# A third PSUM bank in the ring between TensorE and ScalarE, the turned outputs moved into the outputs' bank, and the values read where they were written

## What is computed

```python
q, k, v = to_heads(x @ Wq), to_heads(k), to_heads(v)      # 16 heads, 2048 x 64 each
sim = jnp.einsum('bid,bjd->bij', q, k) * scale
sim = sim + _cope(q, sim, pos_emb)
attn = jax.nn.softmax(sim, axis=-1)
out = jnp.einsum('bij,bjd->bid', attn, v)
return out @ Wout + b_out
```

## Time and profile before

| | |
|---|---|
| median of 3 executions | 2291.75 us (2290.97 to 2293.32) |
| the profiled execution, its own time | 2291.38 us |
| its span in the trace | 2289.5 us |
| busy share of the span: TensorE, ScalarE, VectorE, GpSimd | 97%, 77%, 71%, 17% |
| pairs of the attention | 128, up to about 1856 us of the span |

### The profile page before, as it was taken

The page is one execution under the profiler, slowest core; times in us unless marked ns, Lnnn a source line. Parts: engine busy times, 40 slices in busy tenths (PEclk is TensorE's granted clock), DMA queues, the critical chain, the costliest instruction groups (busy, mean ns, idle before and its releaser), DMA issues. The chain is left out here.

```text
span 2289.5 us, 53196 instructions
## 1 busy us (share of the span) xinstructions
PE 2226.8 (97%) x14577; PEld 1446.7 (63%) x14577; DVE 1633.4 (71%) x4269; ACT 1762.5 (77%) x3723; POOL 389.3 (17%) x673
## 2 busy tenths in 40 slices
PE   7999999999999999999999999999999879999997
PEld 5666666666666666666666666666665547777775
DVE  5888888888888888888888888888888811223232
ACT  5888888888888888888888888888888843455453
POOL 1111111111111111111111111111111101121121
PEclk9999999999999999999999999999999989999998
DMA  2010101010101010101010101010101021010100
GB/s 74 24 40 25 39 24 40 23 39 23 39 25 41 23 40 24 40 23 40 23 39 23 39 23 39 23 40 23 33 14 57 15 67 35 30 39 30 39 30 7
DMA packets 109392, 75.44 MB, mean 33 GB/s; under 512 B 28077, under 2 KB 105070, under 8 KB 109294
## 3 DMA queue, kind: packets, MB, share of 16 engines
q1 hardware_dynamic: 109294, 73.95, 11.6%
HBM read 14.33 MB, written 2.10 MB: 7 GB/s over the span
## 5 line engine op out<-in xcount | busy, mean ns | idle before, releaser
L842 DVE TENSOR_REDUCE mx<-Sc 128x1 f32<-128x1024 f32 (+1 forms) x512 | 568.0, 1130 | 245.1 <-PE Sc L632 244.8
L483 ACT ACTIVATE probsT<-rings 128x512 f32<-128x512 f32 x1024 | 554.1, 594 | 194.6 <-PE rings L640 194.4
L640 PEld LDWEIGHTS rings<-ident,probs 128*128 128x128 f32 x4096 | 437.0, 141 | 304.4 <-issue 103.1
L507 ACT ACTIVATE probs<-Sc,nbias 128x1024 f32<-128x1024 f32 x512 | 566.9, 1112 | 27.9 <-DVE nbias L852 27.9
L640 PE MATMUL rings<-ident,probs 128*128 128x128 f32 x4096 | 566.6, 281 | 3.0 <-ACT probs L507 2.5
L632 PE MATMUL Sc<-qk,q_now 64*128 64x512 f32 x2048 | 531.3, 616 | 10.5 <-ACT probs L507 9.1
L654 PE MATMUL out<-probsT,V_now 128*64 128x256 f32 x4096 | 498.3, 385 | 0.0
L805 DVE COPY_PREDICATED z<-mask,z 128x224 f32<-128x224 int16 (+5 forms) x768 | 393.3, 512 | 11.1
L375 POOL TENSOR_TENSOR prod<-cut,z 128x350 f32<-128x350 f32 x128 | 120.7, 943 | 1466.8 <-DVE z L817 1466.8
L654 PEld LDWEIGHTS out<-probsT,V_now 128*64 128x64 f32 x4096 | 271.4, 136 | 153.6 <-issue 42.5
L632 PEld LDWEIGHTS Sc<-qk,q_now 64*128 64x128 f32 x2048 | 177.5, 186 | 115.9 <-issue 100.6
(11 more groups left out here) (128 smaller groups left out, 2256.8 us busy)
## 6 DMA issues: line engine op xcount, KB each, us to landing
q_now<-qk SPq DMA_DIRECT2D x256, 64.0 KB, 2.0
xv<-xT SPq DMA_DIRECT2D x113, 128.0 KB, 2.2
q_far<-qk SPq DMA_DIRECT2D x256, 32.0 KB, 1.8
V_now<-V SPq DMA_DIRECT2D x16, 512.0 KB, 3.0
at<-attn SPq DMA_DIRECT2D x16, 512.0 KB, 3.2
probs<-in_x_dram SPq DMA_DIRECT2D x4, 512.0 KB, 5.5
wqk<-in_L_attn_Wq_dram SPq DMA_DIRECT2D x32, 64.0 KB, 2.1
xin<-in_x_dram SPq DMA_DIRECT2D x16, 128.0 KB, 2.8
```

The source lines that it names most:

```text
L483: nc.scalar.activation(probsT[:, u, 4 * s:4 * s + 4, :], ring[k % 2][:, :].rearrange("p (t q) -> p t q", q=P), ACT.Copy).then_inc(slot_out, 1)
L507: nc.scalar.activation(probs[:, u, cols], Sc[:, cols], ACT.Exp, bias=nbias[:, u:u + 1], accum_out=sums[:, u, half:half + 1]).then_inc(exp_ ...
L640: last = nc.tensor.transpose(ring[k % 2][:, j * P:(j + 1) * P], probs[:, u, (4 * s + j) * P:(4 * s + j + 1) * P], ident[:, :])
L842: nc.vector.tensor_reduce(mx[:, u, half:half + 1], Sc[:, cols], AX.X, ALU.max).then_inc(dve_unit, 1)
```

## The change

The ring gets the bank of `turns` as its third, and the turned outputs go to columns 256 to 383 of the bank of `out`. `SLOT_BANK` says which bank each of the ten slots uses, and `out_for_bank` how many slots must have been copied out before slot k may be filled. Since the turned outputs and the outputs now share a bank, `outputs(g - 1)` begins only when the turned outputs of the pair g - 2 have been scaled (`scaled`), and ScalarE scales them earlier: between its second and third copy of that group of slots. `V_now`, its copies and the semaphore `v_in` are gone: `outputs` takes its weights straight from `V`. The window waits for slot 4 of the pair in place of slot 5, and only the second transposes of the group behind it wait for `near_out`.

```diff
+SLOT_BANK = [0, 1, 2, 0, 1, 2, 2, 0, 1, 2]
+
+
+def out_for_bank(base, k, late=False):
+
+    if k < 3:
+        return base + ([0, -3, -1] if late else [-2, -1, 0])[k]
+    return base + [1, 2, 3, 6, 4, 5, 7][k - 3]
...
-        V_now = sb("V_now", [P, NT, C])
...
-        rings = pb("rings", [P, 2, BANK])
-        ring = [rings[:, i, :] for i in range(2)]
+        rings = pb("rings", [P, 3, BANK])
+        ring = [rings[:, i, :] for i in range(3)]
         out = pb("out", [P, BANK])
-        turns = pb("turns", [P, BANK])
+        turns = out[:, 2 * P:2 * P + 2 * C]
...
-                if head:
-
-                    wait_apart(sp, out_full, g, waited)
-                    load_values(g)
...
                 if not first:
-                    transposed(1, base, at.last)
+                    transposed(1, base, at.last, (0, 1))
+                    if not second:
+                        scale(g - 2, 0)
+                        scale(g - 2, 1)
+                    transposed(1, base, at.last, (2, 3))
                 exp_half(g, 0, 0)
                 exp_half(g, 0, 1)
-                if not first and not second:
-                    scale(g - 2, 0)
-                    scale(g - 2, 1)
...
-            def transposes(u, base, slots, s):
+            def transposes(u, base, slots, s, late=False):
                 k = slots[s]
-                pe.wait_ge(slot_out, base + k - 1)
+                pe.wait_ge(slot_out, out_for_bank(base, k, late))
...
                     if empty:
                         pe.wait_ge(halves_out, g)
-                    wait_apart(pe, v_in, g // PAIRS * 16 + 16, waited)
+                        wait_apart(pe, scaled, g * 2, waited)
...
-                    last = nc.tensor.matmul(out[half:half + C, 0:2 * P], V_now[:, token_tile(t), :],
+                    last = nc.tensor.matmul(out[half:half + C, 0:2 * P], V[:, keys % 4, token_tile(t), :],
...
                 if far:
-                    wait_apart(pe, slot_out, base + at.now[0], waited)
+                    wait_apart(pe, slot_out, base + at.last[2] + 1, waited)
                     window(g + 2, par if far_par is None else far_par)
...
+                transposes(0, base, at.now, 0)
                 if far:
                     wait_apart(pe, near_out, g * 2 + 6, waited)
-                transposes(0, base, at.now, 0)
                 transposes(0, base, at.now, 1)
```

More of the change, by code:

```diff
@@ L286, in _, with body @@
             weights(1)
-            def load_values(g):
-                sp.dma_start(V_now[:, :, :], V[:, (g // PAIRS) % 4, :, :]).then_inc(v_in, 16)
             sp.wait_ge(slot_out, 8 + 2 * PAIRS)
-            load_values(0)
-            def body(g, odd, late=False, first=False, tile=True, far=True, head=False, near=False):
+            def body(g, odd, late=False, first=False, tile=True, far=True, near=False):
                 base = slots_before(g, late)
@@ L343, in _ @@
             load_early(sp, A, A["ctx_in"])
-            body(LASTP, False, late=True, tile=False, head=True)
+            body(LASTP, False, late=True, tile=False)
             body(LASTP + 1, True, late=True, tile=False)
@@ L412, in _, with project @@
             act.wait_ge(dve_consts, 5)
-            def project(s, odd, base, k, alone=False):
+            def project(s, odd, base, k, bank, alone=False):
                 h, b = s // PAIRS, (s + 7) % PAIRS
                 act.wait_ge(slot_full, base + k + 1)
-                nc.scalar.activation(qk[:, h % 2, int(odd), bass.ds(b // 2 * STEP, STEP)], ring[k % 2][:, 0:STEP],
+                nc.scalar.activation(qk[:, h % 2, int(odd), bass.ds(b // 2 * STEP, STEP)], ring[bank][:, 0:STEP],
                                      ACT.Copy, scale=qk_scale[:, int(odd):int(odd) + 1])\
@@ L533, in body @@
                 if proj:
-                    project(g + PAIRS, not odd, base, at.qk, alone=not val)
+                    project(g + PAIRS, not odd, base, at.qk, SLOT_BANK[at.qk], alone=not val)
                 if val:
@@ L572, in _, with project @@
                 last.then_inc(slot_full, 1)
-            def project(s, odd, base, k, weights_at, alone=False):
+            def project(s, odd, out_before, bank, weights_at, alone=False):
                 b = (s + 7) % PAIRS
                 pe.wait_ge(w_in, weights_at)
-                pe.wait_ge(slot_out, base + k - 1)
+                pe.wait_ge(slot_out, out_before)
                 at = 0 if odd else C
                 for c in range(DC):
-                    last = nc.tensor.matmul(ring[k % 2][:, 0:STEP], wqk[:, c, at:at + 2 * C],
+                    last = nc.tensor.matmul(ring[bank][:, 0:STEP], wqk[:, c, at:at + 2 * C],
                                             xT[:, c, bass.ds(b * STEP, STEP)],
@@ L585, in project, with project_values @@
                 last.then_inc(slot_full, 2 if alone else 1)
[L587 removed]
+            def project_values(s, out_before, bank, ahead=False):
                 if not ahead:
                     pe.wait_ge(xv_in, (s - PAIRS) * 16 + 16)
[L591 removed]
+                pe.wait_ge(slot_out, out_before)
                 for i in range(2 if ahead else 1):
@@ L594, in project_values @@
                         tile = xT[:, c, (2 * s + i) * P:(2 * s + i + 1) * P] if ahead else xv[:, c, :]
-                        last = nc.tensor.matmul(ring[k % 2][:, i * 2 * C:(i + 1) * 2 * C],
+                        last = nc.tensor.matmul(ring[bank][:, i * 2 * C:(i + 1) * 2 * C],
                                                 tile, wv[:, c, :],
@@ L634, in logits, with outputs @@
                 last.then_inc(bank_full, 1)
-            def transposes(u, base, slots, s):
+            def transposes(u, base, slots, s, late=False):
                 k = slots[s]
-                pe.wait_ge(slot_out, base + k - 1)
+                pe.wait_ge(slot_out, out_for_bank(base, k, late))
                 for j in range(4):
-                    last = nc.tensor.transpose(ring[k % 2][:, j * P:(j + 1) * P],
+                    last = nc.tensor.transpose(ring[SLOT_BANK[k]][:, j * P:(j + 1) * P],
                                                probs[:, u, (4 * s + j) * P:(4 * s + j + 1) * P], ident[:, :])
                 last.then_inc(slot_full, 1)
-            def outputs(g, base, slots, tiles, empty=True):
+            def outputs(g, base, slots, tiles, keys, empty=True):
                 if tiles[0] == 0:
@@ L667, in body @@
             def body(g, odd, par, late=False, first=False, proj=True, val=True, far=True, far_par=None,
-                     second=False, new_keys=False):
+                     second=False, new_keys=False, late_before=False, keys=0):
                 base = slots_before(g, late)
@@ L677, in body @@
                 if not first:
-                    transposes(0, base, at.late, 2)
-                    transposes(0, base, at.late, 3)
+                    transposes(0, base, at.late, 2, late_before)
+                    transposes(0, base, at.late, 3, late_before)
                     wait_apart(pe, exp_done, g * 4, waited)
@@ L684, in body @@
                 if not first:
-                    transposes(1, base, at.last, 0)
+                    transposes(1, base, at.last, 0, late_before)
                     transposes(1, base, at.last, 1)
@@ L690, in body @@
                     transposes(1, base, at.last, 3)
-                    outputs(g - 1, base, at.last, range(EARLY_TILES), empty=not second)
+                    outputs(g - 1, base, at.last, range(EARLY_TILES), keys, empty=not second)
                 if far:
-                    wait_apart(pe, slot_out, base + at.now[0], waited)
+                    wait_apart(pe, slot_out, base + at.last[2] + 1, waited)
                     window(g + 2, par if far_par is None else far_par)
@@ L730, in _ @@
             head(LASTP, 1, late=True, proj=False, val=False)
-            body(G - 2, False, 1, late=True, proj=False, val=False, far=False)
-            body(G - 1, True, 1, late=True, proj=False, val=False, far=False)
-            base, at = slots_before(G, True), Slots()
+            body(G - 2, False, 1, keys=H - 1, late=True, proj=False, val=False, far=False, late_before=True)
+            body(G - 1, True, 1, keys=H - 1, late=True, proj=False, val=False, far=False, late_before=True)
+            base, at, late_before = slots_before(G, True), Slots(), True
             pe.wait_ge(exp_done, 4 * G)
-            transposes(0, base, at.late, 2)
-            transposes(0, base, at.late, 3)
-            transposes(1, base, at.last, 0)
+            transposes(0, base, at.late, 2, late_before)
+            transposes(0, base, at.late, 3, late_before)
+            transposes(1, base, at.last, 0, late_before)
             transposes(1, base, at.last, 1)
@@ L741, in _ @@
             transposes(1, base, at.last, 3)
-            outputs(G - 1, base, at.last, range(NT))
-            pe.wait_ge(scaled, 2 * (G - 1))
+            outputs(G - 1, base, at.last, range(NT), H - 1)
             turns_of(G - 1)
```

44 lines of the change are left out of this document (23 added, 21 removed).

## The result

The changed kernel takes 2308.53 us, the median of four executions (2308.16 to 2310.65), against 2291.36 us (2290.72 to 2293.32) before, measured beside it: a ratio of 1.0072, with a 95% interval of 1.0059 to 1.0085. It is slower by 17 us. 2307 us were forecast. The profiled span grew by 16.7 us, from 2289.5 to 2306.2.

What follows compares the result with a forecast made beforehand. TensorE was taken to bound the kernel; outputs waiting for the scalings would cost 124 x 0.125 = 15.5 us, all else nothing, so 2291.75 + 15.5 = 2307 us. The range was 2294 to 2324, the forecast's own 2298 to 2319.

Steps and rivals of the forecast that it cites:

- TensorE sets the pace: First 112 pairs: TensorE busy 599.88 of 600 us, so delaying one of its matmuls lengthens the 14.19 us pair equally.
- The two real waits of the ring: Weight loads for slots 4 and 5 wait for ScalarE's copies; a third bank saves 0.13 us a pair, alone 16 us.
- Only the later of two times counts: Outputs start at the later of transposes done, about 1002.75, and scalings done, 1003.02; the third bank's saving is no separate term.
- The scalings are the later: Chain from turns through ScalarE's scalings to first outputs: 0.14 us late, taken as 0.125 a pair over 124 pairs, 15.5 us.
- 0.40 from turns to scaling: Step from the turns' end to ScalarE's first scaling, with two register instructions behind the wait: taken as 0.40 us.
- its bounds: Turns to first scaling: 0.11 us from the last pair with constant addresses, 0.45 from the projected queries and keys copy.
- The wake-up of TensorE: Step from the end of ScalarE's scalings to TensorE's waiting output matmul: 0.15 us, read from the last pair.
- The removed copies of the values give nothing: The 16 copies of 512 KB are hidden under 6.7 us of other work; removing them gives nothing.
- The rule on banks: Semaphores should guard PSUM by bank, so outputs must wait for scalings; without the rule, a gain of 16 us.
- Rival 1: Scalings done in time, below 0.26 us from turns to first scaling: 0.13 us a pair won, 2276 us; chance 0.13.
- The draw: Rival: scalings ready about when outputs started before, 0.03 us either way, 2288 to 2296 us, named 2292; chance 0.09.
- the longer chain: Rival: costlier TensorE wake-up, or third register instruction separating the scalings: 0.3 us a pair, 2330 us; chance 0.13.

Runs made afterwards that it cites:

- e1: Changed kernel with both scalings writing to one fixed place of attn, so no register instructions precede them: 2285.42 us, ratio 0.9970 to the kernel before.
- e5: Changed kernel with turns one stage earlier, scalings between first and second copy, and two query buffers: 2276.76 us, ratio 0.9935 to the kernel before.
- e2: Changed kernel with the ring of two banks and its old waits: 2306.85 us, ratio 1.0069 to the kernel before.
- e3: Kernel before with only its copies of the values removed, outputs reading them where they were written: 2296.79 us, ratio 1.0021.
- e9: Changed kernel with two buffers for the current queries, loaded a pair ahead: 2301.28 us, ratio 1.0037 to the kernel before.

## Why the prediction was right, and where its sizes were off

- *TensorE sets the pace, so a delay of it lengthens the pair.* Right: 0.09 later outputs in the pair shown, and 0.08 more from pair to pair on average.
- *The two real waits of the ring, worth 0.13 us a pair.* Right: 0.12 in e1 and in e5, as soon as the scalings are early enough.
- *Only the later of two times counts.* Right, and shown most directly by e2: with and without the third bank the pair is 14.27 us.
- *The scalings are the later.* Right in its mechanism. Of its terms, 0.40 from turns to scaling measured 0.41 (996.81 against 996.40), and the 0.52 of both scalings 0.52. The closeness of the 0.40 is partly luck, since neither of its bounds was what I took it for. Of the 0.45 of the nearest copy, 0.28 passed while ScalarE was busy with another (1011.03 + 0.37 = 1011.40, shown under this point), not in register instructions. And 0.11 could not be reached behind the copy of slot 3, which ends 0.29 behind the turns: e1, without register instructions, has 0.21, so they cost 0.20. The wake-up of TensorE was over-sized: 0.15, taken from the last pair, where 0.09 was measured. Hence 0.08 in place of 0.125 a pair, 10 us in place of 15.5.

```profile
1011.03 0.37 ACT L499 ACTIVATE halves<-out 128x256 f32<-128x256 f32 x1
```

- *The removed copies of the values give nothing.* This step failed. Their removal cost 5 us in e3, through late loads of queries, and about 8 us of the change's 17 by e9. I had argued from the outputs, which do not wait for the copy, and not looked at the load with the least slack in the pair. That the total came out within 2 us of the forecast is luck: the scalings cost 6 less than forecast, and the late loads, forecast at nothing, about 8.
- *The rule on banks.* By the Trainium skill, "PSUM — Partial Sum Buffer", section "PSUM bank collisions raise a hardware error", the wait for the scalings cannot be left out. No run has the shared bank without the wait, so none shows the rule itself. What the runs add is the price of the wait in this kernel: 0.08 us a pair where the turns come late, and nothing in e5, where they come early.
- *The rivals.* Rival 1, the scalings in time, is what e1 makes true by taking the register instructions out: the prediction put the border at 0.26 us from turns to scaling, and 0.21 gives a gain, 0.41 the loss. The draw and the longer chain did not happen.

## What to carry to other kernels

A freed buffer is worth its wait only if nothing else holds the same instruction: ask for each added wait what will be the later of the two, and move the producer first. Here two matmuls and the scalings behind them, issued one stage earlier, turned a loss of 0.08 us a pair into a gain of 0.12. Count the register instructions behind a wait as a part of the chain as soon as they lose their cover, and for every load in a loop know how much later than its median it may land.

## What the runs showed of the hardware that was not expected

- With one 0.02 MB fetch of program code in the same 3.8 us as two 64 KB loads, their median landing was 2.6 us in place of 2.0, and the logits that needed them waited 0.69 us.
- The register instructions of ScalarE's two scalings, 37 to 213 ns each, put the first scaling 0.41 us behind the turns in place of 0.21.
- TensorE's first matmul behind a wait for ScalarE started 0.09 us after the end of the scaling in the loop, and 0.15 behind a copy at the end of the attention.
